# Routed experts as 48 pairs of 64-row half blocks on two column tiles of TensorE, in place of 63 blocks of 128 rows

## The chip, the cores and the metric

One core of one Trainium2 chip runs the kernel as one program. The metric is the device time of one execution in microseconds (us), as the median of several runs. In the profile the engines are PE (TensorE; PEld is its loading of stationary operands), DVE (VectorE), ACT (ScalarE), POOL (GpSimd) and SP (SyncE, which here issues DMAs).

## The reference

The model has two layers, each an attention part and a feed-forward part with layer norms around them, over 1024 tokens (2 x 512) of 256 features in fp32. The change touches only the last part, a mixture of experts:

```python
logits = x @ gate_w                              # 1024 x 32
topw, topi = jax.lax.top_k(softmax(logits), 4)   # 4 of 32 experts per token
topw = topw / topw.sum(-1, keepdims=True)
for each expert e:                               # wg, wu: 256 x 96; wd: 96 x 256
    h = silu(x @ wg[e]) * (x @ wu[e])
    out += combine[:, e:e+1] * (h @ wd[e])
out += sigmoid(x @ seg) * (silu(x @ sg) * (x @ su)) @ sd
```

So there are 1024 x 4 = 4096 pairs of a token and an expert, spread unevenly over 32 experts. How many fall to an expert is known only at run time.

## The kernel before, in words

The program is written engine by engine: each engine has its own list of instructions in program order, and semaphores tie the lists together (`wait_ge` before, `then_inc` after an instruction). `Chain.step` and `Chain.settle` (lines 57 to 80) make an engine wait for its own earlier results. Nothing is scheduled by a planner; the order in each list is the order of the source.

Up to about 488 us of the profile come the first layer, the second attention part, routing and the shared expert. Routing has these pieces. `route_top` takes the four best experts of each token. On TensorE `ranks` counts, for each token and expert, how many tokens come before it at that expert, and the totals. On VectorE `route_places` (L1224, once for each batch of 512 tokens) turns ranks and totals into a row number in the buffer `x_sorted` for each of the four copies of a token; `block_experts` (L1284) works out which expert each block of 128 rows belongs to, and this table goes through TensorE (`block_row`, L2051) into one row `etab` from which registers can be loaded. GpSimd scatters each token's row (256 features and 12 columns that say where the result is to go) four times into `x_sorted` (`scatter`, L779), after SP has filled that buffer with padding rows. Rows of one expert fill whole blocks of 128, so that 4096 / 128 + 31 = 63 blocks are enough for every distribution, and always 63 are run.

The stage of the blocks, in which the change lies, does this for each block i:

- SP (L605 to L610) loads 128 rows of 268 floats into `xblk`, four blocks ahead; it waits until the block four before is transposed and its ids are taken.
- TensorE `block_in` (L2057): two transposes of 128 x 128 into PSUM.
- VectorE `block_in` (L1354): copies the columns to `xcol` (L1359), and a small step (L1361) that finds which of the row's four copies this is; `block_ids` (L1365) reduces that to the row number `ids`.
- TensorE `block_up` (L2070): two matmuls (k = 0, 1), stationary `xcol` 128 x 128, moving the expert's 192 columns of `wgu`, at an address from a register. In fp32 each matmul is two instructions in the trace. The register is loaded by `value_load` (L2169), one block at a time.
- ScalarE `block_silu` (L1679) and VectorE `block_gate` (L1371) make the 128 x 96 hidden rows `hb`.
- TensorE `block_hidden` (L2084) transposes them, VectorE `block_hidden` (L1379) copies them to `hcol` (L1384).
- TensorE `block_down` (L2090): one matmul, stationary `hcol` 96 x 128, moving the expert's 256 columns of `wd`.
- ScalarE `block_out` (L1687) copies the result to `yblk`; GpSimd (L806 to L812) scatters its rows to `y_slots` by `ids`.

In one turn of its loop TensorE does `block_in(i)`, `block_up(i-1)`, `block_hidden(i-2)`, `block_down(i-3)`, and VectorE `block_in(i)`, `block_gate(i-1)`, `block_ids(i)`, `block_hidden(i-2)`. PSUM and SBUF tiles of a block are doubled (`i % 2`), and waits such as `pe.wait_ge(bt_copied, i - 1)` guard their reuse. After the last block the results are read back (`ycomb`), weighted and summed (`combine`, L1397).

The functions that the diff touches and what calls them:

## Time and profile before

| | us |
|---|---|
| median of 3 runs | 618.08 |
| runs | 617.88 to 623.02 |
| span of the profiled execution (first to last instruction) | 634.5 |
| of it, TensorE busy | 467.0 (74%) |
| of it, VectorE busy | 377.9 (60%) |
| of it, ScalarE busy | 263.8 (42%) |
| of it, GpSimd busy | 231.8 (37%) |

The profiled execution is another one than the timed runs; of it only the span is given. Busy times are sums over the span, and the kernel's stages have different limits, so a stage is read from its own window. Ends of matmuls are modelled in the trace, and a busy TensorE is not one at its peak. "<-" names what ended the idle time before an instruction; "issue" is time in which an engine waited for nothing that the profile shows.

### The profile page before, as it was taken

To read this page: it belongs to the slowest core of one execution; us is meant where nothing else is said; L and a number is where in the kernel's file an instruction comes from. 1 tells how busy PE (TensorE), PEld (TensorE's weight loads), DVE (VectorE), ACT (ScalarE), POOL (GpSimd) and SP (SyncE) were. 2 spreads that over 40 slices of the span, in tenths; PEclk is the share of its full clock that TensorE was granted. 3 is DMA by queue.
4 is the path that set the end of the run, shared out by engine and by line. 5 is a ranking of instruction groups with operands and counts; after the bars stand their busy time and mean duration, and the time that the engine had idled before them with its cause. 6 is when DMAs were issued, how large, how long until landed. Compare 5 with 4: busy or idle time off the path is not lost.

```text
span 634.5 us, 9931 instructions
## 1 busy us (share of the span) xinstructions
PE 467.0 (74%) x3183; PEld 342.9 (54%) x3183; DVE 377.9 (60%) x940; ACT 263.8 (42%) x507; POOL 231.8 (37%) x310
## 2 busy tenths in 40 slices
PE   2766888889886689798944445596785999999650
PEld 1544444444543377676734334484664878877440
DVE  6584577775671347655498839863712656665254
ACT  7317665664676342316711451423312434433202
POOL 5940323432548303203102211265170456565500
PEclk9957598996997769898987666997896999999776
DMA  6680521111410159300000006983022444543061
GB/s 191 156 164 22 84 44 40 39 31 30 143 38 3 67 161 337 110 1 1 1 1 25 25 25 141 256 251 113 18 104 61 125 133 126 150 137 98 11 265 66
DMA packets 56050, 60.16 MB, mean 95 GB/s; under 512 B 10420, under 2 KB 46909, under 8 KB 56000
## 3 DMA queue, kind: packets, MB, share of 16 engines
q1 hardware_dynamic: 50832, 50.79, 30.6%
q0 software_dynamic: 5168, 8.74, 4.1%
q8 instruction: 27, 0.44, 0.3%
q14 instruction: 23, 0.19, 0.1%
HBM read 37.67 MB, written 25.75 MB: 100 GB/s over the span
## 4 chain that ended last, share of the span: by engine, by line
PE 51%; DVE 21%; ACT 10%; issue 8%; DMA 4%; POOL 2%; another core or an unknown queue 2%; SPq 1%; POOLq 0%; DVEq 0%; ACTq 0%
PE ps L2076 8%; PE ps L1820 6%; PE ps L1799 5%; PE ps L2095 4%; PE ps L1870 4%; PE ps L1778 4%; ACT probs L1505 3%; PE ps L1858 3%; PE ps L1860 3%; PE ps L1859 3%; PE ps L2066 3%; DVE gain L1104 2%; DVE st L902 2%; PE ps L1832 2%; DVE h_lo L1061 2%
## 5 line engine op out<-in xcount | busy, mean ns | idle before, releaser
L1505 ACT ACTIVATE probs<-ps 128x512 f32<-128x512 f32 x160 | 86.9, 595 | 61.5 <-PE ps L1799 59.7
L809 POOL DMA_INDIRECT y_slots_scratch<-yblk,ids x63 | 62.0, 985 | 62.5 <-issue 28.8
L998 DVE TENSOR_REDUCE negm<-ps 128x2 f32<-128x1024 f32 (+1 forms) x64 | 67.1, 1080 | 26.3 <-PE ps L1788 26.1
L653 POOL TENSOR_TENSOR rstd<-ve,halfneg 128x4 f32<-128x4 f32 x16 | 16.6, 1036 | 132.0 <-DVE ve L933 79.6
L2076 PE MATMUL ps<-wgu,xcol 128*128 x252 | 58.5, 356 | 2.8 <-DVE xcol L1359 1.1
L1778 PE MATMUL ps<-k_all,q_ring 64*128 64x512 f32 (+3 forms) x256 | 52.9, 420 | 8.1 <-DVE negm L998 4.7
L1799 PE MATMUL ps<-q_ring,k_all 64*128 64x512 f32 (+3 forms) x256 | 44.2, 404 | 17.5 <-ACT probs L1505 17.5
L1820 PE MATMUL ps<-probs,v_all 128*32 128x128 f32 (+3 forms) x512 | 51.1, 499 | 5.2 <-POOL probs L698 2.8
L2076 PEld LDWEIGHTS ps<-wgu,xcol 128*128 128x128 f32 x252 | 40.3, 193 | 11.2 <-issue 8.4
L1545 ACT CAST h_hi<-hf 128x512 fp32r<-128x512 f32 x28 | 17.4, 620 | 66.7 <-DVE hf L1056 58.1
L1799 PEld LDWEIGHTS ps<-q_ring,k_all 64*128 64x128 f32 x256 | 23.3, 210 | 40.1 <-ACT probs L1505 30.2
L690 POOL TENSOR_TENSOR waited<-zero 128x1 f32<-128x1 f32 x48 | 9.3, 195 | 92.6 <-ACT probs L1505 92.6
L784 POOL DMA_INDIRECT x_sorted_scratch<-rows,dest x32 | 32.0, 1000 | 25.9 <-DVE dest L1282 16.7
L1778 PEld LDWEIGHTS ps<-k_all,q_ring 64*128 64x128 f32 x256 | 28.4, 218 | 23.7 <-issue 12.7
L1056 DVE TENSOR_TENSOR hf<-sg,ps 128x512 f32<-128x512 f32 x28 | 19.2, 684 | 36.5 <-PE ps L1860 13.2
L1001 DVE TENSOR_REDUCE negm<-ps 128x4 f32<-128x1024 f32 (+1 forms) x32 | 30.5, 959 | 16.0 <-PE ps L1788 15.9
L698 POOL TENSOR_SCALAR_AFFINE_SELECT probs<-probs 128x512 f32<-128x512 f32 x64 | 40.0, 637 | 0.0
L2095 PE MATMUL ps<-wd,hcol 96*128 x126 | 39.6, 398 | 0.4 <-DVE hcol L1384 0.3
L1376 DVE TENSOR_TENSOR hb<-gb,ps 128x96 f32<-128x96 f32 x63 | 16.0, 253 | 35.5 <-ACT gb L1684 23.6
L1684 ACT ACTIVATE gb<-ps 128x96 f32<-128x96 f32 x63 | 15.8, 251 | 45.0 <-PE ps L2076 37.1
L1359 DVE COPY xcol<-ps 128x256 f32<-128x256 f32 x63 | 26.6, 422 | 12.6 <-PE ps L2066 12.0
L1692 ACT COPY yblk<-ps 128x256 f32<-128x256 f32 x63 | 23.4, 372 | 23.9 <-PE ps L2095 19.6
(291 smaller groups left out, 1306.5 us busy)
## 6 DMA issues: line engine op xcount, KB each, us to landing
x_sorted_scratch<-pad SPq DMA_DIRECT2D x7, 1206.0 KB, 13.6
xblk<-x_sorted_scratch SPq DMA_DIRECT2D x63, 134.0 KB
wgu<-in_moe_w SPq DMA_DIRECT2D x4, 1536.0 KB
q_ring<-q_parts_scratch SPq DMA_DIRECT2D x64, 64.0 KB
ycomb<-y_slots_scratch SPq DMA_DIRECT2D x8, 512.0 KB, 7.0
wd<-in_moe_w SPq DMA_DIRECT2D x1, 3072.0 KB, 19.1
sraw<-in_moe_w SPq DMA_DIRECT2D x6, 384.0 KB, 3.5
q_parts_scratch<-qparts SPq DMA_DIRECT2D x4, 512.0 KB, 4.6
```

The lines of the kernel that those rows point to most:

```text
L698: pool.affine_select(out=tiles, in_=tiles, compare_op=ALU.is_ge, fill=0.0, base=0, pattern=[[0, GQ], [1, P]], channel_multiplier=-1).then_ ...
L784: pool.indirect_dma_start(out=x_sorted, out_offset=bass.IndirectOffsetOnAxis(ap=dest[:, u, j:j + 1], axis=0), in_=rows[:, u, :], in_offset ...
L809: pool.indirect_dma_start(out=y_slots, out_offset=bass.IndirectOffsetOnAxis(ap=ids[:, i:i + 1], axis=0), in_=yblk[:, i % YR, :], in_offset ...
L998: dve.tensor_reduce(negm[:, par, :, hp, qt], pair_of, AX.X, ALU.max, negate=True).then_inc(s1_read, 1)
L1001: dve.tensor_reduce(negm[:, par, :, :, qt], pair_of.rearrange("p a (h t) -> p a h t", h=nh), AX.X, ALU.max, negate=True).then_inc(s1_read, 1)
L1359: dve.tensor_copy(xcol[:, i % 2, :], ps[:, i % 2, 0:D]).then_inc(bt_copied, 1)
L1505: act.activation(probs[:, par, u, :], ps[:, col_unit(g, u), :], ACT.Exp)\
L1778: pe.matmul(ps[:, u % 2 * 2 + rg, end - w:end], q_ring[lane(rg, 64), g % QRING, h0 + h, qt * P:(qt + 1) * P], k_all[lane(rg, 64), g * T:g ...
L1799: mm = pe.matmul(ps[:, col_unit(g, 2 * p + rg), c:c + w], k_all[lane(rg, 64), g * T + kt * P:g * T + (kt + 1) * P], q_ring[lane(rg, 64), g ...
L1820: mm = pe.matmul(ps[32 * h:32 * h + 32, 7, kt * P:T], v_all[:, (g * TPB + kt) * 32:(g * TPB + kt + 1) * 32], probs[:, g % 2, un, c:c + T - ...
L2076: mm = pe.matmul(ps[:, 2 + i % 2, 0:2 * F].rearrange("p (w f) -> p w f", w=2), xcol[:, i % 2, k * P:(k + 1) * P], wgu[:, k, :, bass.ds(e * ...
L2095: pe.matmul(ps[:, 4 + i % 2, 0:D], hcol[0:F, i % 2, :], wd[0:F, bass.ds(e, 1), :].rearrange("p o d -> p (o d)"), start=True, stop=True).th ...
```

## The change

The unit of the buffer becomes a half block of 64 rows, and two half blocks make a pair that goes through the stage as a block did. Each of the 32 experts has one half block of its own, at a place known when the program is written; what an expert has beyond 64 rows goes to 64 free half blocks, whose experts are known at run time (`etab`). That is 96 half blocks, 48 pairs. Pair i has free half block i in rows 0 to 63. In rows 64 to 127 it has, for two pairs of three, the own half block of a fixed expert (`own_expert`), and for every third pair one of the last 16 free ones, whose weights ScalarE copies ahead to a fixed place (`copy_weights`).

- SP issues two loads of 64 rows for a pair (`first_rows`); padding takes 6 DMAs in place of 7.
- `block_up` and `block_down` on TensorE issue one matmul for each half: the stationary operand has 64 columns, the result goes to 64 partitions. The last pair has one expert and keeps the full width.
- Registers of four free half blocks are loaded at once, after `block_in` of every fourth pair. Waits that other waits imply are dropped.
- The order of a turn becomes, on TensorE, `block_in(i)`, (loads), `block_hidden(i-3)`, `block_up(i-1)`, `block_down(i-3)`, and on VectorE `block_in(i)`, `block_hidden(i-3)`, `block_gate(i-2)`, `block_ids(i)`; on ScalarE `block_silu(i-1)`, `block_out(i-3)`.
- `route_places` compares with 15 limits in place of 8 and has more steps (`to_own` among them).

The diff without its declarations, allocations and iotas, but for those of names that matter:

```diff
-BLOCKS = N * TOPK // P + E - 1
+HB = P // 2
+LIMITS = N // HB - 1
+FREE = N * TOPK // HB
+BLOCKS = (E + FREE) // 2
+TRIOS = BLOCKS // 3
...
+        def own_expert(i):
+            return None if i % 3 == 2 else i // 3 * 2 + i % 3
+        def first_rows(i):
+            own = own_expert(i)
+            return E * HB + i * HB, (E + BLOCKS + i // 3) * HB if own is None else own * HB
...
-                sp.dma_start(xblk[:, i % XR, :], x_sorted[i * P:(i + 1) * P, :])\
-                    .then_inc(xb_in[i % XR], 16)
+                for n, first in enumerate(first_rows(i)):
+                    sp.dma_start(xblk[half(n), i % XR, :], x_sorted[first:first + HB, :])\
+                        .then_inc(xb_in[i % XR], 16)
...
+            def to_own(rank):
+                chain.step(dve.scalar_tensor_tensor(
+                    pos[:, :, :], rank, float(HB),
+                    own[:, :].unsqueeze(1).to_broadcast((P, TPB, E)), ALU.is_lt, ALU.mult))
...
                 chain.step(dve.tensor_tensor(
-                    over[:, :, :], total.unsqueeze(2).to_broadcast((P, E, 8)),
-                    thr[:, :].unsqueeze(1).to_broadcast((P, E, 8)), ALU.is_gt))
+                    over[:, :, :], total.unsqueeze(2).to_broadcast((P, E, LIMITS)),
+                    thr[:, :].unsqueeze(1).to_broadcast((P, E, LIMITS)), ALU.is_gt))
                 if b == 1:
                     chain.step(dve.tensor_tensor(
                         late[:, :, :], rank, lim0[:, :].unsqueeze(1).to_broadcast(grid),
                         ALU.is_ge))
+                    to_own(rank)
                 chain.settle()
                 nb = (nb0, nb1)[b]
                 chain.step(dve.tensor_reduce(nb[:, :], over[:, :, :], AX.X, ALU.add))
...
                 if b == 0:
                     chain.step(dve.tensor_tensor_scan(in0[:, :], onesE[:, :], nb0[:, :], 0.0,
                                                       ALU.mult, ALU.add))
-                    chain.step(dve.tensor_scalar(lim0[:, :], nb0[:, :], float(P), None, ALU.mult))
-                    chain.settle()
-                    chain.step(dve.tensor_tensor(ex0[:, :], in0[:, :], nb0[:, :], ALU.subtract))
+                    chain.step(dve.tensor_scalar(lim0[:, :], nb0[:, :], float(HB), float(HB),
+                                                 ALU.mult, ALU.add))
                     chain.settle()
                     chain.step(dve.scalar_tensor_tensor(
-                        pos[:, :, :], ex0[:, :].unsqueeze(1).to_broadcast(grid), float(P), rank,
-                        ALU.mult, ALU.add))
+                        ex0[:, :], in0[:, :], float(E - 1), nb0[:, :], ALU.add, ALU.subtract))
+                    chain.settle()
+                    chain.step(dve.tensor_tensor(own[:, :], iota[:, :], ex0[:, :], ALU.subtract))
+                    chain.settle()
+                    to_own(rank)
+                    chain.settle()
+                    chain.step(dve.tensor_tensor(
+                        late[:, :, :], pos[:, :, :], ex0[:, :].unsqueeze(1).to_broadcast(grid),
+                        ALU.add))
                 else:
                     chain.step(dve.tensor_tensor(nb1[:, :], nb1[:, :], nb0[:, :], ALU.subtract))
                     chain.settle()
...
                         late[:, :, :], late[:, :, :],
                         ex0[:, :].unsqueeze(1).to_broadcast(grid), ALU.add))
                     chain.settle()
-                    chain.step(dve.scalar_tensor_tensor(
-                        pos[:, :, :], late[:, :, :], float(P), rank, ALU.mult, ALU.add))
+                    chain.step(dve.tensor_tensor(late[:, :, :], late[:, :, :], pos[:, :, :],
+                                                 ALU.add))
+                chain.settle()
+                chain.step(dve.scalar_tensor_tensor(
+                    pos[:, :, :], late[:, :, :], float(HB), rank, ALU.mult, ALU.add))
                 chain.settle()
                 shape = (P, TPB, TOPK, E)
...
-            for i in range(BLOCKS + 2):
+            for i in range(BLOCKS + 3):
                 if i < BLOCKS:
                     block_in(i)
-                if 0 <= i - 1 < BLOCKS:
-                    block_gate(i - 1)
+                if 0 <= i - 3 < BLOCKS:
+                    block_hidden(i - 3)
+                if 0 <= i - 2 < BLOCKS:
+                    block_gate(i - 2)
                 if i < BLOCKS:
                     block_ids(i)
-                if 0 <= i - 2 < BLOCKS:
-                    block_hidden(i - 2)
...
+            def copy_weights(c, e):
+                act.copy(wcopy[:, c % 2, :, :, :], wgu[:, :, :, bass.ds(e * F, F)])
+                act.copy(wdcopy[0:F, c % 2, :],
+                         wd[0:F, bass.ds(e, 1), :].rearrange("p o d -> p (o d)"))\
+                    .then_inc(w_copied, 1)
+            act.wait_ge(etab_ready, 1)
+            act.wait_ge(s_wd, 16)
+            act.wait_ge(s_wgu, 64)
+            for i in range(BLOCKS + 3):
+                if i % 8 == 1 and 8 <= i <= 33:
                     diagonal(*divmod(i // 8 - 1, 2))
-                if i < BLOCKS:
-                    block_silu(i)
-                if i >= 2:
-                    block_out(i - 2)
+                c = i // 3
+                if i % 3 == 0 and c < TRIOS - 1:
+                    copy_weights(c, act.value_load(etab[0:1, BLOCKS + c:BLOCKS + c + 1],
+                                                   min_val=0, max_val=E - 1))
+                if 0 <= i - 1 < BLOCKS:
+                    block_silu(i - 1)
+                if 0 <= i - 3 < BLOCKS:
+                    block_out(i - 3)
...
             def block_in(i):
-                pe.wait_ge(xb_in[i % XR], 16 * (i // XR + 1))
-                if i >= 2:
-                    pe.wait_ge(bt_copied, i - 1)
-                else:
+                pe.wait_ge(xb_in[i % XR], 32 * (i // XR + 1))
+                if i == 0:
                     pe.wait_ge(silu_done, B * (HC + SHARED))
                     pe.wait_ge(mul_done, B * (HC + SHARED))
                 for k in range(DC):
...
             def block_up(i, e):
+                own, c = own_expert(i), i // 3
                 pe.wait_ge(bt_copied, i + 1)
-                if i >= 2:
-                    pe.wait_ge(b_mul, i - 1)
+                if own is None and c < TRIOS - 1:
+                    pe.wait_ge(w_copied, c + 1)
                 for k in range(DC):
-                    mm = pe.matmul(
-                        ps[:, 2 + i % 2, 0:2 * F].rearrange("p (w f) -> p w f", w=2),
-                        xcol[:, i % 2, k * P:(k + 1) * P], wgu[:, k, :, bass.ds(e * F, F)],
-                        start=k == 0, stop=k == DC - 1)
+                    cols = xcol[:, i % 2, k * P:(k + 1) * P]
+                    up = ps[:, 2 + i % 2, 0:2 * F].rearrange("p (w f) -> p w f", w=2)
+                    free = wgu[:, k, :, bass.ds(e * F, F)]
+                    if i == BLOCKS - 1:
+                        mm = pe.matmul(up, cols, free, start=k == 0, stop=k == DC - 1)
+                    else:
+                        second = (wcopy[:, c % 2, k, :, :] if own is None
+                                  else wgu[:, k, :, own * F:(own + 1) * F])
+                        pe.matmul(up[half(0)], cols[:, half(0)], free, start=k == 0,
+                                  stop=k == DC - 1)
+                        mm = pe.matmul(up[half(1)], cols[:, half(1)], second, start=k == 0,
+                                       stop=k == DC - 1)
                 mm.then_inc(bu_done, 1)
             def block_hidden(i):
                 pe.wait_ge(b_mul, i + 1)
-                if i >= 2:
-                    pe.wait_ge(bh_copied, i - 1)
                 pe.transpose(ps[0:F, 6 + i % 2, 0:P], hb[:, i % 2, :], ident[:, :])\
                     .then_inc(bh_done, 1)
             def block_down(i, e):
+                own, c = own_expert(i), i // 3
                 pe.wait_ge(bh_copied, i + 1)
                 if i >= 2:
                     pe.wait_ge(by_ready, i - 1)
-                pe.matmul(ps[:, 4 + i % 2, 0:D], hcol[0:F, i % 2, :],
-                          wd[0:F, bass.ds(e, 1), :].rearrange("p o d -> p (o d)"),
-                          start=True, stop=True).then_inc(bd_done, 1)
+                free = wd[0:F, bass.ds(e, 1), :].rearrange("p o d -> p (o d)")
+                if i == BLOCKS - 1:
+                    mm = pe.matmul(ps[:, 4 + i % 2, 0:D], hcol[0:F, i % 2, :], free,
+                                   start=True, stop=True)
+                else:
+                    pe.matmul(ps[half(0), 4 + i % 2, 0:D], hcol[0:F, i % 2, half(0)], free,
+                              start=True, stop=True)
+                    mm = pe.matmul(ps[half(1), 4 + i % 2, 0:D], hcol[0:F, i % 2, half(1)],
+                                   wdcopy[0:F, c % 2, :] if own is None else wd[0:F, own, :],
+                                   start=True, stop=True)
+                mm.then_inc(bd_done, 1)
...
             for i in range(BLOCKS + 3):
                 if i < BLOCKS:
                     block_in(i)
+                    if i % 4 == 0:
+                        _, loaded = nc.values_load_multi_w_load_instructions(
+                            etab[0:1, i:i + 4], engines=[mybir.EngineType.PE], min_val=0,
+                            max_val=E - 1)
+                        experts.update(enumerate(loaded, i))
+                if 0 <= i - 3 < BLOCKS:
+                    block_hidden(i - 3)
                 if 0 <= i - 1 < BLOCKS:
-                    experts[i - 1] = pe.value_load(etab[0:1, i - 1:i], min_val=0, max_val=E - 1)
                     block_up(i - 1, experts[i - 1])
-                if 0 <= i - 2 < BLOCKS:
-                    block_hidden(i - 2)
                 if 0 <= i - 3 < BLOCKS:
                     block_down(i - 3, experts.pop(i - 3))
...
```

## Rows read from the trace of the kernel before

**Rows 1.** Page, first line and busy times in 40 slices of the span.
```profile
span 634.5 us, 9931 instructions
...
PE   2766888889886689798944445596785999999650
...
PEclk9957598996997769898987666997896999999776
```
**Rows 2.** Chain that ended last, 480 to 600 us: start us, us, what.
```profile
488.25 0.42 PE ps L2066 x2
488.70 0.43 DVE xcol L1359
...
489.35 1.64 PE ps L2076 x4
...
577.14 1.56 PE ps L2066 x2
...
583.34 1.54 PE ps L2087
...
594.42 0.97 PE ps L2076 x4
...
598.41 0.38 ACT yblk L1692
```
**Rows 3.** Timeline of one block: start us, us, engine, line, operation, count.
```profile
540.58 0.38 PE L2066 MATMUL ps<-ident,xblk 128*128 128x128 f32 x2
...
540.92 0.91 PE L2076 MATMUL ps<-wgu,xcol 128*128 x4
...
541.00 0.42 DVE L1359 COPY xcol<-ps 128x256 f32<-128x256 f32 x1
541.34 0.21 DVE L1361 SCALAR_TENSOR_TENSOR xblk<-xblk,placf 128x4 f32<-128x4 f32 x1
...
541.67 0.27 PE L2087 MATMUL ps<-ident,hb 128*96 128x128 f32 x1
...
541.78 0.60 PE L2095 MATMUL ps<-wd,hcol 96*128 x2
...
542.21 0.38 PE L2066 MATMUL ps<-ident,xblk 128*128 128x128 f32 x2
```
**Rows 4.** Busy time in a window: PE, PEld, DVE, ACT, POOL, clock, DMA, GB/s.
```profile
520.00:560.00 40.00, 39.42 (x224) 32.45 (x224) 25.40 (x123) 17.33 (x58) 24.20 (x26) 1.00 0.52 140
```
**Rows 5.** Attention: timeline of TensorE, then L1820 and L1778 there, ns min/median/max.
```profile
102.04 0.86 PE L1820 MATMUL ps<-probs,v_all 128*32 128x256 f32 x16
102.83 0.50 PE L1778 MATMUL ps<-k_all,q_ring 64*128 64x512 f32 x2
...
L1820 PE MATMUL ps<-probs,v_all x16: 272/326/403, 102.0 to 102.6; 128*32 128x256 f32 x8, 128*32 128x128 f32 x8
...
L1778 PE MATMUL ps<-k_all,q_ring x4: 386/445/497, 102.8 to 103.6; 64*128 64x512 f32 x4
```
**Rows 6.** Timeline, a down product that waited, and VectorE's steps one behind another.
```profile
584.75 0.31 PE L2087 MATMUL ps<-ident,hb 128*96 128x128 f32 x1
...
584.90 0.29 DVE L1384 COPY hcol<-ps 96x128 f32<-96x128 f32 x1
...
585.33 0.69 PE L2095 MATMUL ps<-wd,hcol 96*128 x2 [0.27 <-DVE hcol L1384]
...
585.67 0.42 DVE L1359 COPY xcol<-ps 128x256 f32<-128x256 f32 x1 [0.48 <-remote]
...
586.01 0.21 DVE L1361 SCALAR_TENSOR_TENSOR xblk<-xblk,placf 128x4 f32<-128x4 f32 x1
...
586.18 0.25 DVE L1376 TENSOR_TENSOR hb<-gb,ps 128x96 f32<-128x96 f32 x1
```
**Rows 7.** Line L2169 on TensorE's sequencer: ns min/median/max, first and last start.
```profile
L2169 PEldq TENSOR_LOAD <-etab x63: 296/303/522, 488.4 to 593.6; - x63
...
L2169 PEldq SEQ_ASSERT  x63: 18/18/28, 489.2 to 594.1; - x63
```
**Rows 8.** Chain that ended last: the first step of each route_places.
```profile
390.99 0.43 DVE over L1231
...
450.83 0.33 DVE over L1231
```
**Rows 9.** Groups by form on VectorE, 450 to 457 us: busy us, mean ns.
```profile
L1275 DVE TENSOR_TENSOR eq<-eq,pos 128x512 f32<-128x512 f32 x1 | 0.7, 691 | 0.0
...
L1231 DVE TENSOR_TENSOR over<-ps,thr 128x256 f32<-128x256 f32 x1 | 0.4, 416 | 0.0
```
**Rows 10.** Single lines: ns min/median/max; and one group of the page (mean ns).
```profile
L1692 ACT COPY yblk<-ps x63: 360/372/378, 494.4 to 598.4; 128x256 f32<-128x256 f32 x63
...
L609 SPq DMA_DIRECT2D xblk<-x_sorted_scratch x63: 319/319/433, 478.2 to 586.6; - x63
...
L1505 ACT ACTIVATE probs<-ps 128x512 f32<-128x512 f32 x160 | 86.9, 595 | 61.5 <-PE ps L1799 59.7
```

More of the change, by code:

```diff
@@ L228, in sandwich_kernel @@
         wgu_at = mhi_at - 2 * E * F * 4
+        (wcopy, wdcopy), end = place(
+            region, ("wcopy", [P, 2, DC, 2, F], F32), ("wdcopy", [P, 2, D], F32))
+        assert end <= half_q
         (wgu,), _ = place(wgu_at, ("wgu", [P, DC, 2, E * F], F32))
@@ L798, in _ @@
                 chunk_low(c)
[L799 removed]
+            pool.wait_ge(s_sorted, 6 * 16)
             scatter(0)
@@ L1210, in block_constants @@
             def block_constants():
-                dve.wait_ge(s_const2, 6)
+                dve.wait_ge(s_const2, 7)
                 chain.step(dve.memset(rows[:, :, D + TOPK:XW], 0.0))
-                chain.step(dve.tensor_copy(placf[:, :], placi[:, :]))
+                chain.step(dve.tensor_scalar(placf[half(0), :], placi[half(0), 0:BLOCKS],
+                                             float(E * HB), None, ALU.add))
+                second = placf[half(1), :].rearrange("p (g m) -> p g m", m=3)
+                chain.step(dve.tensor_scalar(
+                    second[:, :, 0:2],
+                    placi[half(1), BLOCKS:].rearrange("p (g m) -> p g m", m=3)[:, :, 0:2],
+                    float(-HB), None, ALU.add))
+                chain.step(dve.tensor_scalar(second[:, :, 2], placi[half(1), 0:TRIOS],
+                                             float((E + BLOCKS - 1) * HB), None, ALU.add))
                 chain.settle()
```

43 lines of the change are left out of this document (24 added, 19 removed).

## The prediction

> **What bounds the kernel now.** I read the chain of waits first, then the timeline of one block, then the windows by stage. The chain passes through the routed experts from 488.25 us (first transposes of block 0) to 598.41 us (last copy of an output block): 110 of 634.5 us, and in it nearly every step is TensorE's [rows 1, 2]. From the first block's up product (489.35) to the last one's (594.42) lie 62 blocks in 105.1 us, 1.69 us each. One block undisturbed is 540.92 to 542.48, 1.56 us: up product 0.75 to the next instruction, the transpose of the hidden rows 0.11, the down product 0.43, the two transposes of the next block 0.27 [rows 3]. So 62 x 1.56 = 96.7 us are the pace of TensorE and 8.4 us are not: they sit in the cold first blocks and in some ten places where a step of the chain takes 1 to 1.5 us instead of 0.3 (577.14 and 583.34 are two) [rows 2]. In 520 to 560 TensorE is busy 39.42 of 40 us at clock 1.00, VectorE 25.40, ScalarE 17.33, GpSimd 24.20 [rows 4]. TensorE is what a block costs; the others have room.
>
> **The change, step 1: fewer passes.** 48 pairs replace 63 blocks. At 1.56 us each that would take away 15 x 1.56 = 23.4 us. This is the most that the change can give, and it holds only if a pair costs what a block costs.
>
> **Step 2: do two halves of 64 columns run side by side?** A pair issues twice the matmuls for the up and the down product. The trace has fp32 column tiles already: in attention (L1820) 16 instructions of four 32-column tiles, 8 of width 256 and 8 of width 128, begin at 102.04, and the next work begins at 102.83 [rows 5]. A 256-wide instruction streams in 0.215 (two downs take 0.43 [rows 3]), so one after another they would need 8 x 0.215 + 8 x 0.107 = 2.6 us; they took 0.7 to 0.8. Four ran at once. I take two halves as side by side: up 4 x 0.162 = 0.65, down 2 x 0.215 = 0.43, as now. Not side by side they would add 0.65 + 0.43 = 1.08 us a pair.
>
> **Step 3: what a pair adds on TensorE.** Column tiles alternate with full-width transposes, twice a pair. In the same place the work after the column tiles begins 0.07 us before the modelled end (102.04 + 0.86) of the last of them; that one is 128 wide, lasts 0.27 as recorded, streams 0.107, so 0.10 us pass with nothing streaming. Then its weights have to be loaded in the open: L1778 lasts 497 ns there against 386 in the middle of its run, 0.11 us for 128 columns [rows 5]; for 64 columns I estimate half, 0.055, and for a transpose 0.05 (the hidden transpose that waited lasts 0.31 against 0.27 [rows 3, 6]). TensorE alone: three transposes 0.05 + 0.33, gap 0.10, up 0.055 + 0.65, down 0.43, gap 0.10: 1.72 us.
>
> **Step 4: the wait that takes over.** The new order is transposes(i), hidden(i-3), up(i-1), down(i-3) on TensorE, and on VectorE columns(i), ids step, hidden copy(i-3), gate(i-2), ids(i). The down product now waits for a hidden copy made in the same turn, and VectorE makes that copy only behind the column copy, which waits for the turn's transposes. Before, hidden copy and down product were one turn apart. The loop, from the turn's start: second transpose begins at 0.16, its recorded end is 0.27 later (0.43); the column copy begins 0.04 after that (540.96 to 541.00), 0.47; the next VectorE step 0.34 later, 0.81; the one behind it 0.17 later, which is the hidden copy, 0.98 [rows 3, 6]; from the start of a hidden copy to the down product that waited for it are 0.43 (584.90 to 585.33) [rows 6], 1.41; weights 0.055, first of the two rounds 0.215, so the last begins at 1.68; the next turn's transposes begin 0.07 before its recorded end of 0.38, at 1.99. So a pair costs 1.99 us and not 1.72: TensorE is ready for the down product at 1.19 and waits 0.22. Behind the waiting product stand the next transposes, and VectorE waits for those: that is why the wait is paid in full.
>
> **Step 5: register loads.** Now every block reads its expert's number (L2169): a load of 0.30 us, an operation of 0.15 and a check, 0.5 us from the load's start to the check in the last block, 0.8 in the first [rows 7]; it passes while TensorE works off what is queued. The change loads four at a time, after the transposes of every fourth pair and ahead of the hidden transpose. The queue behind it is free when the down product of the turn before has been let go, at about 1.41, and the hidden transpose may come as late as 0.62 into the next turn without delaying the hidden copy (0.98 less 0.04, 0.27 and 0.05), so 1.99 + 0.62 - 1.41 = 1.20 us are free. What four cost the trace doesn't show: at least one (0.5), at most four in a row (4 x 0.8 = 3.2). I take one load and four times the rest of it at an estimated 0.27: 1.4 us, 0.2 over, 12 times: 2.4 us. At the low end 0, at the high end 12 x 2.0 = 24 us.
> The Trainium skill (Runtime: NRT & Kernel Launch, Instruction fetch mechanics) gives about 200 ns for each register loaded, in bulk too. By it the four would need 0.8 us of loading instead of 0.30, and the sum would be 12 x 0.5 = 6 us higher. No run here shows more than one register in a load; the one that the rows show took 0.30.
>
> **Step 6: ahead of the stage.** Both calls of route_places lie on the chain (from 390.99 and 450.83) [rows 8]. Limits go from 8 to 15: the comparison and its sum go from 256 to 480 elements; 0.42 us at 256 and 0.69 at 512 [rows 9] make 0.24 more each, 0.475 per call. The first call gets three more dependent steps (one of 32 elements, 0.2; two of 128, 0.3 each, with the settle between them 0.86); the second one step beside another (0.2) and one dependent (0.32). Together 1.33 + 1.0 = 2.3 us, all on the path: the table of experts and the destinations wait for it.
>
> **Step 7: what I cost at nothing.** ScalarE copies weights for every third pair: 384 elements, between 0.37 (256) and 0.60 (512) [rows 10], 0.37 more, and a register load; some 1.5 us on every third turn beside 0.25 + 0.37 each turn, against 1.99, and the gate has a turn's slack more than before. Without that cover it would cost 15 x 0.2 = 3 us. VectorE's five steps last 1.32 us of 1.99. GpSimd's scatter (0.98) comes 48 times in place of 63. SP issues 96 loads of 64 rows at 0.32 each [rows 10], 0.64 a turn, four turns ahead. The removed waits on TensorE free its queue, which the wait of step 4 makes worth nothing.
>
> **The sum.** 47 turns x 1.99 = 93.5, and 2.4 for register loads: 95.9 against 96.7. I leave the 8.4 us of irregular time and the stage's ends as they are: 104.3 against 105.1, -0.8. With +2.3 ahead of it: +1.5 us. The profiled execution, whose span is 634.5, would come to 636.0; only its span is given, and it is 16.4 us above the median of the runs (618.08), so some of its stalls may be the profiler's. On the median: 619.6.
>
> **The rivals.**
> A, faster: the hidden copy is not waited for, and TensorE's own 1.72 us sets the pace. For it: VectorE has 0.67 us free in a turn, and some turns may find columns copied early. Against it: the order on VectorE is fixed. 47 x 1.72 = 80.8; the register loads then find less cover (0.93 free, 12 x 0.47 = 5.6): 86.4 + 8.4 + 2.3 against 105.1 is -8.0: 610.
> B, faster: the irregular 8.4 us shrink with 15 fewer scatters and shorter loads. All of it gone: 611.
> C, slower: four loads cost four times one. At 0.65 each, 2.6 us: 1.4 over, 12 times 16.8 in place of 2.4: 634. It decides from about 1.8 us per group of four, where the total is +1%.
> D, slower: the halves run side by side only in part (the two instructions of one half hold up the next half): up 0.82 and down 0.64, some 0.2 us more a turn: 629. If not at all, 47 x 0.8 more: 657, against rows 5.
> E, slower: each late step now meets a loop without slack and costs twice: +8: 628.
>
> **How the numbers follow.** Within 1% (a measurement of this kernel can tell about 1%, 6 us, from no change): my forecast, 0.50. A 0.13 and B 0.07: faster 0.20. C 0.15, D 0.08, E 0.07: slower 0.30. The forecast's own range, from a turn of 1.93 to 2.08 and 0 to 6 us of register loads, is 615 to 627. The range given takes in A and B and reaches up to C: 608 to 634; outside are a full A with less irregular time, D without any overlap, and the high end of step 5.
>
> **What would show it.** Right: in the stage the turn is 1.9 to 2.1 us; TensorE's idle time before the first instruction of the down product is put down to the hidden copy, in nearly every turn; up instructions start in twos some ns apart; the full clock holds. Step 5: every fourth turn longer by some tenths. Step 6: the stage begins 2 to 3 us later if nothing else moves. Wrong: a turn of 1.75 (A) or over 2.3 (C, D), up products of 0.8 us and more, a clock below 1.00 within the stage, ScalarE's copies ahead of the gate as what VectorE waits for.

## The result

Over 20 runs each, the changed kernel takes 622.02 us against 619.60 us for the kernel before on the same chip; the ratio is 1.0045, with a 95% interval of 1.0023 to 1.0067. The forecast was 619.6 us and "within 1%". Medians here and below are of all runs, ratios leave the slow ones out (here two of the changed kernel, at 628 and 629 us). The profiled execution of the kernel before, on which the prediction rests, has a span of 634.5 us [rows 1]; another execution of the same kernel (first experiment below) has 618.2. The profiled execution of the changed kernel takes 620.25 us and has a span of 618.5.

The page of the changed kernel, first line and slices, answers to [rows 1]; its window answers to [rows 4], with the same columns:

```profile
span 618.5 us, 9821 instructions
...
PE   2766888898886779798965244777777899999650
...
PEclk9957599999898769898996576898789899999866
```
```profile
520.00:560.00 40.00, 36.71 (x289) 19.27 (x285) 19.19 (x97) 18.32 (x58) 18.68 (x19) 1.00 0.39 107
```

In the same window TensorE is busy 36.71 us in place of 39.42, VectorE 19.19 in place of 25.40, GpSimd 18.68 in place of 24.20. These three have more room than before, ScalarE (18.32 in place of 17.33) is still idle more than half the time, the granted clock is 1.00, and yet the stage takes no less time: something that is no engine's load sets the pace. One turn, in the timeline of the changed kernel (start us, us, engine, line, operation), answers to [rows 3]:

```profile
506.75 0.44 PE L2132 MATMUL ps<-ident,xblk 128*128 128x128 f32 x2
...
507.02 0.27 PE L2160 MATMUL ps<-ident,hb 128*96 128x128 f32 x1
...
507.22 0.42 DVE L1412 COPY xcol<-ps 128x256 f32<-128x256 f32 x1 [1.09 <-PE ps L2132]
507.23 0.38 PE L2151 MATMUL ps<-wgu,xcol 128*64 x1
...
507.23 0.38 PE L2153 MATMUL ps<-wgu,xcol 128*64 128x192 f32 x1
...
507.56 0.21 DVE L1414 SCALAR_TENSOR_TENSOR xblk<-xblk,placf 128x4 f32<-128x4 f32 x1
...
507.70 0.28 DVE L1437 COPY hcol<-ps 96x128 f32<-96x128 f32 x1
...
507.76 0.33 PE L2151 MATMUL ps<-wgu,xcol 128*64 x1
...
508.11 0.13 PEld L2174 LDWEIGHTS ps<-wd,hcol 96*64 96x64 f32 x1 [0.36 <-issue]
508.12 0.42 PE L2174 MATMUL ps<-wd,hcol 96*64 x1
...
508.70 0.33 PE L2132 MATMUL ps<-ident,xblk 128*128 128x128 f32 x1
```

A turn is 506.75 to 508.70, 1.95 us. The reader is to follow the loop: transposes, column copy at 507.22, the small step at 507.56, the hidden copy at 507.70, and only then, at 508.12, the down product (L2174), though the last up instruction (L2151) began at 507.76 and the rounds of an up product follow one another in 0.16. The view puts the idle time of the weight load down to "issue" and not to the hidden copy; the order of the starts points to the wait, and an experiment below (hidden copy first) shows it.

Every fourth turn is longer. These rows are the turn with the register load, then the load's line on TensorE's sequencer (ns min/median/max), which answers to [rows 7]:

```profile
512.60 0.44 PE L2132 MATMUL ps<-ident,xblk 128*128 128x128 f32 x2
...
513.58 0.31 PE L2160 MATMUL ps<-ident,hb 128*96 128x128 f32 x1 [0.54 <-issue]
...
514.52 0.38 PE L2174 MATMUL ps<-wd,hcol 96*64 x1
...
515.05 0.44 PE L2132 MATMUL ps<-ident,xblk 128*128 128x128 f32 x2
```
```profile
L2251 PEldq FUSED_REGOPS  x48: 146/148/165, 480.1 to 571.8; - x48
...
L2251 PEldq TENSOR_LOAD <-etab x12: 328/332/533, 479.5 to 570.6; - x12
```

The hidden transpose comes 0.98 after the transposes in place of 0.27, and the turn lasts 2.45. Eleven turns are of this kind, 2.43 to 2.62, 2.52 in the mean; the others are 1.95 from the fourth on. The 47 intervals make 98.0 us.

### The profile page after: what moved, and what is told of

The parts are those of the page before. It is cut to its first block, busy times and chain, and to the rows that moved or that the text cites. A ratio compares the mean times of both kernels' runs of the same rounds, so it can differ in the third digit from the quotient of the medians.

```text
span 618.5 us, 9821 instructions
## 1 busy us (share of the span) xinstructions
PE 450.1 (73%) x3330; PEld 305.7 (49%) x3330; DVE 364.1 (59%) x872; ACT 266.8 (43%) x507; POOL 217.9 (35%) x296
## 4 chain that ended last, share of the span: by engine, by line
PE 47%; DVE 21%; issue 11%; ACT 10%; POOL 7%; DMA 3%; SPq 1%; POOLq 0%; DVEq 0%; ACTq 0%
PE ps L2151 6%; PE ps L1888 6%; PE ps L1867 5%; PE ps L2174 4%; PE ps L1846 4%; POOL x_sorted_scratch L812 4%; ACT probs L1558 3%; PE ps L2132 3%; PE ps L1938 3%; PE ps L1926 2%; DVE st L930 2%; PE ps L1927 2%; PE ps L1928 2%; PE ps L1900 2%; DVE gain L1132 2%
## 5 line engine op out<-in xcount | busy, mean ns | idle before, releaser
L837 POOL DMA_INDIRECT y_slots_scratch<-yblk,ids x48 | 47.2, 984 | 64.0 <-ACT yblk L1745 56.9
L1888 PE MATMUL ps<-probs,v_all 128*32 128x128 f32 (+3 forms) x512 | 48.4, 476 | 5.7 <-DVE att L1054 2.9
L1412 DVE COPY xcol<-ps 128x256 f32<-128x256 f32 x48 | 20.4, 424 | 53.7 <-PE ps L2132 53.7
L2151 PE MATMUL ps<-wgu,xcol 128*64 x188 | 41.9, 347 | 0.0
L1089 DVE TENSOR_TENSOR h_lo<-hf,h_hi 128x512 fp32r<-128x512 f32 x28 | 20.9, 745 | 19.2 <-ACT h_hi L1598 16.5
L1852 PE MATMUL ps<-hide_swap,swapped 64*128 64x128 bf16 x128 | 31.7, 247 | 0.0
L1852 PE MATMUL ps<-hide_cols,identb 64*128 64x128 bf16 x128 | 31.7, 247 | 0.0
L2174 PE MATMUL ps<-wd,hcol 96*64 x94 | 29.6, 397 | 1.2 <-DVE hcol L1437 0.5
L1737 ACT ACTIVATE gb<-ps 128x96 f32<-128x96 f32 x48 | 11.9, 247 | 41.9 <-PE ps L2153 26.8
```

Source lines behind the costliest of these rows:

```text
L837: pool.indirect_dma_start(out=y_slots, out_offset=bass.IndirectOffsetOnAxis(ap=ids[:, i:i + 1], axis=0), in_=yblk[:, i % YR, :], in_offset ...
L1852: pe.matmul(ps[:, u % 2 * 2 + rg, end - P:end], own[lane(rg, 64), :], masks[lane(rg, 64), :], start=False, stop=False)
L1888: mm = pe.matmul(ps[32 * h:32 * h + 32, 7, kt * P:T], v_all[:, (g * TPB + kt) * 32:(g * TPB + kt + 1) * 32], probs[:, g % 2, un, c:c + T - ...
L2151: pe.matmul(up[half(0)], cols[:, half(0)], free, start=k == 0, stop=k == DC - 1)
L2174: pe.matmul(ps[half(0), 4 + i % 2, 0:D], hcol[0:F, i % 2, half(0)], free, start=True, stop=True)
```

## The experiments

All times are medians, ratios are against the kernel before on the same chip. "Stage" is the time from the first transpose of the stage to the end of the last copy of an output block; a turn or interval is the time from one block's transposes to the next one's.

| run | us | ratio [95%] | stage us | turn us |
|---|---|---|---|---|
| before, again (first) | 619.97 (one run) | | 103.0 | 1.54 median, 1.58 mean |
| changed kernel | 622.02 | 1.0045 [1.0023, 1.0067] | 104.7 | 1.95, with load 2.52 |
| hidden copy first | 614.54 | 0.9934 [0.9911, 0.9958] | 96.5 | 1.71, with load 2.3 to 2.8 |
| single loads | 615.93 | 0.9932 [0.9897, 0.9966] | 98.3 | 1.95 |
| both | 610.62 | 0.9853 [0.9784, 0.9922] | 92.9 | 1.83 mean |
| whole blocks | 615.94 | 0.9922 [0.9878, 0.9967] | 99.3 | 1.84, with load 2.3 to 2.7 |
| before, fewer waits | 611.86 | 0.9862 [0.9782, 0.9942] | 94.9 | 1.42 median, 1.45 mean |
| load ahead | 605.84 | 0.9746 [0.9679, 0.9813] | 88.8 | 1.71, 1.75 mean |
| half after half | 622.27 (one run) | | 105.1 | 1.95 |
| whole, load ahead | 596.53 | 0.9659 [0.9602, 0.9716] | 79.4 | 1.49 median, 1.55 mean |
| two per switch | 632.01 | 1.0143 [1.0074, 1.0212] | 112.1 | 3.1 to 7.5 for two |
| two per switch, deep | 602.43 | 0.9709 [0.9683, 0.9735] | 82.5 | 3.12 for two |

**The kernel before once more**, unchanged.

> The kernel before, unchanged, for a second profile. My theory: its late steps (8.4 us in the stage) and the 10.6 us stall ahead of the stage belong to that one profiled execution; then the span is about 616 to 618, the stage of the blocks begins at about 480 (set by the scatter of rows, not by the shared expert) and lasts about 102 us at 1.56 to 1.60 us a block. Rival: they belong to the kernel; then the span is again over 630 and the 62 intervals take 105 us.

Stage 478.77 to 581.77, 103.0 us, against 110.5 in the profile on record (488.25 to 598.79 [rows 2]). The 62 intervals take 98.0 us, not 105.1. The irregular 8.4 us of the prediction belonged mostly to that one execution: 98.0 against 96.7 leaves 1.3 us of it. And 62 intervals of before now cost exactly what 47 turns of after cost, 98.0 us.

**Is it the hidden copy that the down product waits for?** The hidden copy is put ahead of the column copy on VectorE, nothing else:

```diff
             for i in range(BLOCKS + 3):
-                if i < BLOCKS:
-                    block_in(i)
                 if 0 <= i - 3 < BLOCKS:
                     block_hidden(i - 3)
+                if i < BLOCKS:
+                    block_in(i)
```

> The changed kernel with one move on VectorE: the hidden copy of pair i-3 stands ahead of the column copy of pair i in a turn. My theory (step 4: the down product waits for a hidden copy that stands behind the column copy): the hidden copy begins at 0.58 in the turn and not at 0.98, the down product is ready at 1.01, TensorE is not before 1.19, so three turns of four go from 1.955 to about 1.72. The turn with the four register loads keeps less cover and is longer by some 0.8 and not 0.55: a group of four takes 7.7 us and not 8.37, 8 us in all: about 614. Rival: the pace is set elsewhere (drains between tile modes, ScalarE's copies): the group stays at 8.4 and the time at 622.

The timeline of one turn of it:

```profile
508.18 0.44 PE L2132 MATMUL ps<-ident,xblk 128*128 128x128 f32 x2
...
508.76 0.29 DVE L1437 COPY hcol<-ps 96x128 f32<-96x128 f32 x1 [0.73 <-PE ps L2160]
...
508.97 0.41 DVE L1412 COPY xcol<-ps 128x256 f32<-128x256 f32 x1
...
509.36 0.38 PE L2174 MATMUL ps<-wd,hcol 96*64 x1
...
509.89 0.44 PE L2132 MATMUL ps<-ident,xblk 128*128 128x128 f32 x2
```

The hidden copy now starts 0.58 after the transposes in place of 0.95, the down product 1.18 in place of 1.37, and the turn is 1.71 to the hundredth. Two exchanged steps on an engine that is half idle give 8.2 us of stage. The load turns now stand out more, since the flat turn covers less.

**What do four registers at once cost?** The load of one number at a time, ahead of its up product, as in the kernel before:

```diff
-                    if i % 4 == 0:
-                        _, loaded = nc.values_load_multi_w_load_instructions(
-                            etab[0:1, i:i + 4], engines=[mybir.EngineType.PE], ...)
-                        experts.update(enumerate(loaded, i))
                 if 0 <= i - 1 < BLOCKS:
+                    experts[i - 1] = pe.value_load(etab[0:1, i - 1:i], min_val=0, max_val=E - 1)
                     block_up(i - 1, experts[i - 1])
```

> The changed kernel with its registers loaded one at a time, directly ahead of the up product, as before the change. My theory (step 5): one load with its check takes 0.72 us on TensorE's queue and has 0.9 to 1.0 us of cover there (from the release of the down product at 1.41 to the up product at 2.4), so every turn is 1.955 and the 0.55 us in every fourth turn are gone: 12 x 0.55 = 6.6 us, about 615.5. Rival: loads cost by their number wherever they stand, 48 x 0.3 us or more are added: over 630.

Every turn is 1.95 from the fourth on and none longer: 48 single loads cost nothing that shows, 12 fourfold ones the 6.3 us by which the stage is now shorter. The sequencer's records in the changed kernel show why (start us, ns, what, without the checks of 18 ns; line L2174 is the down product before, L2151 the up product behind):

```
511.918  46 FUSED_REGOPS L2174
512.058 330 TENSOR_LOAD  L2251
512.446 151 FUSED_REGOPS L2251
512.732 151 FUSED_REGOPS L2251
...
513.298 146 FUSED_REGOPS L2251
513.599  51 FUSED_REGOPS L2151
```

The load begins when the down product is let go, 1.41 after the turn's start (510.65). The load itself takes 0.33 us for four numbers, against 0.30 for one [rows 7]; each number then costs 0.28 more on the sequencer. In all it is 1.51 us until the hidden transpose's weights at 513.57.

**Both edits together.**

> Both moves together. My theory: every turn at TensorE's own 1.72 us, flat: 47 x 1.72 = 81 us in place of 98, about 604 to 605, below the kernel before. Rival: one of the two covers is used up by the other (the load of 0.72 ends at 1.74, the up product is wanted at 2.1), or another engine sets the pace at 1.9: 611 or more.

It missed: 610.62 and a mean turn of 1.83. The two gains use one cover. With a turn of 1.71 a load between the hidden transpose and the up product starts only when the gate is through, and the up product begins 0.20 to 0.48 us after the hidden transpose in place of 0.20 to 0.24.

**The load ahead of the hidden transpose**, still one number a turn (the edit is against the version with both edits):

```diff
+                if 0 <= i - 1 < BLOCKS:
+                    experts[i - 1] = pe.value_load(etab[0:1, i - 1:i], min_val=0, max_val=E - 1)
                 if 0 <= i - 3 < BLOCKS:
                     block_hidden(i - 3)
                 if 0 <= i - 1 < BLOCKS:
-                    experts[i - 1] = pe.value_load(etab[0:1, i - 1:i], min_val=0, max_val=E - 1)
                     block_up(i - 1, experts[i - 1])
```

> The changed kernel with the hidden copy ahead of the column copy on VectorE, and with one register loaded in each turn, ahead of the hidden transpose and not behind it. Theory: in the run with both edits the load stood behind the wait of the hidden transpose (released at about 1.49 of a turn of 1.71), so 0.72 us of loading ended after the up product could have started. Ahead of the hidden transpose it begins when the down product is let go, at 0.87, and ends at 1.6, before the hidden transpose is due at 1.98: every turn 1.71 to 1.75, stage 87 to 89 us, 604 to 606 us. Rival (the sequencer has too much to issue in 1.71 us wherever the load stands): turns of 1.80 and more, 609 to 611 us, as with the load behind.

605.84 us, stage 88.8, nearly every turn 1.71: against the version with both edits only the place of the load differs, so the place decided there. Against "hidden copy first" only the grouping differs, one number a turn in place of four every fourth turn at the same place, and the stage is 88.8 in place of 96.5 us: the grouping costs by itself. This version does all the work of the changed kernel and beats both: 0.9746 of before.

**Do the halves run side by side because they alternate?** The up product's instructions are ordered first half k = 0, 1, then second half k = 0, 1 in place of by turns.

> The changed kernel, with the up product's instructions in the order first half k = 0, first half k = 1, second half k = 0, second half k = 1, in place of alternating halves. Result and work are the same. It asks how the halves come to run side by side. Theory 1 (each tile is fed on its own, so the second half's stream starts without waiting for the first half's): nothing changes, turn 1.95, 622 us. Theory 2 (instructions start in order, so the second half begins only when the first half's last one streams): the up product takes seven rounds of 0.162 in place of four, 1.13 us, and ends 0.27 us behind the time at which the down product could start: turn about 2.2, some 13 us more: 635 us.

```profile
509.10 0.38 PE L2149 MATMUL ps<-wgu,xcol 128*64 x1
509.12 0.38 PE L2155 MATMUL ps<-wgu,xcol 128*64 128x192 f32 x1
509.31 0.33 PE L2149 MATMUL ps<-wgu,xcol 128*64 x1
509.33 0.33 PE L2155 MATMUL ps<-wgu,xcol 128*64 128x192 f32 x1
```

L2149 is the first half, L2155 the second, in this run's timeline: though all of L2149 stands ahead of L2155 in the list, they start 0.02 us apart and pass each other. Nothing changed in the time.

**What do the two tiles cost?** Each pair as one whole block, so the second half's own expert is left out:

```diff
-                    if i == BLOCKS - 1:
+                    if True:
                         mm = pe.matmul(up, cols, free, start=k == 0, stop=k == DC - 1)
...
-                if i == BLOCKS - 1:
+                if True:
                     mm = pe.matmul(ps[:, 4 + i % 2, 0:D], hcol[0:F, i % 2, :], free, ...)
```

> The changed kernel, but each of the 48 pairs is multiplied as one whole block of 128 rows: one instruction of 128 columns in place of two halves of 64, in the up and in the down product. The second half's own expert is left out (its rows go through the first half's expert). Waits, register loads, copies and transfers stay. It prices the two column tiles. Theory (the loop of step 4 sets the turn; the tiles cost it only what stands behind the down product): the down product still starts at about 1.37 to 1.40 us of the turn, lasts 0.43, and no 0.10 us of drain follows it: turn 1.82 in place of 1.95, every fourth again 0.55 longer, stage some 6 us shorter: about 616 us. Rival 1 (the tiles cost nothing): turn 1.95, 622. Rival 2 (the tiles are what makes a pair slower than a block): turn 1.56, about 603.

The turn fell to 1.84 and the time to 615.94, as the theory had it:

```profile
531.25 0.38 PE L2132 MATMUL ps<-ident,xblk 128*128 128x128 f32 x2
...
532.14 0.28 DVE L1437 COPY hcol<-ps 96x128 f32<-96x128 f32 x1
...
532.56 0.69 PE L2171 MATMUL ps<-wd,hcol 96*128 x2 [0.17 <-DVE hcol L1437]
...
533.09 0.38 PE L2132 MATMUL ps<-ident,xblk 128*128 128x128 f32 x2
```

Whole blocks still wait for the hidden copy, and here the view names it. So of the 0.4 us by which a pair's turn is longer than a block's the halves make 0.11; the most of it is the loop through VectorE.

The same edit in the version with the load ahead, where TensorE itself sets the turn:

> The version with the hidden copy first and one register load a turn ahead of the hidden transpose, but with each pair multiplied as one whole block of 128 rows (the second half's own expert is left out). It prices the two column tiles where TensorE itself sets the turn. Theory: the halves cost 1.71 less 1.42, the interval that 63 whole blocks reached without the spare waits: some 0.29 us a pair for draining twice and loading the first weights in the open. Turn 1.42 to 1.45, stage about 76 us, 592 us. Rival (with 1.42 us VectorE or the sequencer is the bound at once, so the tiles cost less than 0.29 in truth): turn 1.55 to 1.65, 597 to 602 us.

596.53 us, median turn 1.49, between the two: the tiles cost at least 0.22 us a pair there. It need not be all, since a part of the 1.49 is TensorE's list and not its array: every third turn takes 1.55, and these are the turns in whose list stands the wait for ScalarE's copied weights (L2141), which takes 0.05 us and 0.106 until the next step. At a turn of 1.71 or 1.95 the same wait doesn't show. Against 63 blocks at 1.42 (the next experiment) the price would be 0.29.

**What were the removed waits worth by themselves?** In the kernel before, with its 63 blocks, the three waits that the change also takes out:

```diff
-                if i >= 2:
-                    pe.wait_ge(bt_copied, i - 1)
-                else:
+                if i < 2:
...
-                if i >= 2:
-                    pe.wait_ge(b_mul, i - 1)
...
-                if i >= 2:
-                    pe.wait_ge(bh_copied, i - 1)
```

> The kernel before, with 63 blocks, without the three waits on TensorE that the change takes out as well (columns copied in block_in, gate multiplied in block_up, hidden copied in block_hidden, each from i = 2). It tells what that part of the change is worth by itself. Theory: before, TensorE's sequencer is short of time: a register load every block and seven waits; the streamed work of a block is about 1.45 us and the interval 1.54 to 1.58. Without the three waits the interval falls to 1.45 to 1.50: 62 times 0.1, some 6 us: 613 us. Rival (waits already passed cost nothing, as step 7 of the prediction has it): the interval stays 1.54 to 1.58, 619 us.

611.86 us, 0.9862 of before, and most intervals are 1.42. The timeline of one block of it, against 540.58 to 542.21 in [rows 3]:

```profile
540.36 0.38 PE L2064 MATMUL ps<-ident,xblk 128*128 128x128 f32 x2
540.58 0.81 PE L2072 MATMUL ps<-wgu,xcol 128*128 x4
541.23 0.27 PE L2081 MATMUL ps<-ident,hb 128*96 128x128 f32 x1
541.34 0.60 PE L2089 MATMUL ps<-wd,hcol 96*128 x2
541.77 0.38 PE L2064 MATMUL ps<-ident,xblk 128*128 128x128 f32 x2
```

The up product now takes 0.65 to the next instruction, not 0.75. In the unchanged kernel these waits stand on the sequencer as follows (one of the three, ns min/median/max):

```profile
L2074 PEldq EVENT_SEMAPHORE  x61: 51/51/51, 483.4 to 578.1; - x61
```

Each is implied by an earlier wait in the same list and so can't hold anything up, but each takes 0.05 us and some 0.11 to 0.125 until the next step of the list. Some 0.12 of the 1.54 us of a block were thus the list and not the array. This part of the change, alone and with 63 blocks, is faster than the whole change (0.9862 of before against 1.0045).

**Half as many changes of tiling.** The version with the load ahead, with two pairs in a turn and one load of two numbers: four transposes and two hidden transposes on the whole array, then two up and two down products in halves; VectorE and ScalarE go in twos, and `xcol` has four buffers.

```diff
-            for i in range(BLOCKS + 3):
+            for g in range(0, BLOCKS + 4, 2):
...
+                    block_in(g)
+                    block_in(g + 1)
...
+                    block_hidden(g - 4)
+                    block_hidden(g - 3)
...
+                    block_up(g - 2, experts[g - 2])
+                    block_up(g - 1, experts[g - 1])
...
+                    block_down(g - 4, experts.pop(g - 4))
+                    block_down(g - 3, experts.pop(g - 3))
```

> The same version, with two pairs in each turn: four transposes and two hidden transposes on the whole array, then two up and two down products in halves, so that TensorE changes between whole array and column tiles half as often; VectorE and ScalarE take their steps in twos, the columns have four buffers in place of two, and one load brings two registers. Theory: each change of tiling costs about 0.14 us (drain and open weight load), so a pair costs 0.14 less: double turn of 3.13 us, 24 of them, stage some 7 us shorter: 598 to 600 us. Rival 1 (the 0.29 us are paid by each half product, not by the change): double turn 3.42, 606 us. Rival 2 (the longer chain through VectorE and ScalarE, or the two-register load, takes the place): double turn over 3.5, 608 us and more.

None of the three: 632.01, slower than before. The transposes' line names a cause (us of idle time, times, weight loads and matmuls counted apart):

```profile
  DMA xblk<-x_sorted_scratch: 22.8, 27
```

The matmuls alone are 13 of the 27, with 11.3 us, 3.8 of it ahead of the stage; in the chain that ended last, transfers of rows and their issue on SP make 34% of 480 to 593 us. A turn takes two blocks of rows at once, the buffers hold four, and a new load starts only when the ids of a block four back are taken. Besides, behind a late transpose the load of two numbers holds up the hidden transposes (idle before them, "issue", 11.2 us in 16 times). Seven buffers, ids ahead of the gates, and two single register loads (one ahead of the down products) mend it together; what each of the three does alone was not run:

> The version with two pairs a turn once more, with what held it up taken away: seven input buffers in place of four (TensorE waited for input rows at 27 transposes), the token numbers worked out ahead of the gates on VectorE, and two single register loads a turn, one ahead of the down products, one behind the transposes, in place of one load of two. Theory (each change of tiling costs some 0.14 us, and the last run was slow for its transfers alone; its undisturbed double turns were 3.12): double turn 3.12 to 3.2, stage some 83 us, 599 to 601 us. Rival (the chain through VectorE and ScalarE or the register loads still set the turn): double turn 3.4 to 3.6, 606 to 612 us.

```profile
530.75 0.66 PE L2130 MATMUL ps<-ident,xblk 128*128 128x128 f32 x4
531.55 0.48 DVE L1436 COPY hcol<-ps 96x128 f32<-96x128 f32 x2 [1.01 <-PE ps L2158]
...
532.90 0.38 PE L2172 MATMUL ps<-wd,hcol 96*64 x1
...
533.87 0.66 PE L2130 MATMUL ps<-ident,xblk 128*128 128x128 f32 x4
```

The double turn is 3.12 from one end of the stage nearly to the other, 1.56 a pair in place of 1.71. If the saved changes of tiling were all that the grouping saves, two changes would cost 0.30 us, near the 0.29 above and over the 0.22; buffers and loads differ too, so 0.22 to 0.30 is what the runs show. The time, 602.43, is 1.4 us above the upper end expected, though the stage of 82.5 us is as expected. It is the fastest version here with the whole computation.

## Why the prediction was right, point by point

**What bounds the kernel** was half right. TensorE set the pace of a block, but in part by its list of instructions and not by its array: without three waits that were already passed a block takes 1.42, not 1.54. So the pairs were set against a block that could itself be 0.12 faster, and a pair of 1.56 or 1.71 is never as cheap as such a block, though 47 turns of 1.56 still take less than 62 intervals of 1.42 (73 against 88 us).

**Steps 1 and 2** hold. 15 passes fewer came, and the halves run side by side: starts 0.01 apart, and the rounds of an up product follow one another in 0.16 as before.

**Step 3** holds: TensorE alone was put at 1.72 and is 1.71 where nothing waits (hidden copy first). Its part for the tiles, two gaps of 0.10 and weights in the open, is 0.22 to 0.30 by the runs with whole blocks and with two pairs in a turn. The Trainium skill (TensorEngine Tiling (Array Packing), Tiling Modes) has it that a change of tiling mode drains the array, without a price; the price of a change that the runs show here fits it.

**Step 4** carried the forecast and holds: turn 1.95 for 1.99, down product at 1.37 for 1.41, put down to the order on VectorE, which the exchange of two steps showed. The sign named for it failed in part: the views of the changed kernel call most of this idle time "issue".

**Step 5 is the term that was mis-sized**: "1.4 us, 0.2 over, 12 times: 2.4 us". The load begins at 1.41 as told and lasts 1.51, near 1.4. The cover was wrong: "the hidden transpose may come as late as 0.62 into the next turn" looks at VectorE alone. Behind the hidden transpose stands the up product, and TensorE had only the 0.22 us of step 4 to spare, so the transpose may come 0.27 + 0.22 = 0.49 into the turn. The cover is then 1.95 + 0.49 - 1.41 = 1.03 in place of 1.20, and 1.51 is 0.48 over; the eleven turns are 0.57 longer in the mean, 6.2 us, where 2.4 was told for twelve (the first load falls into the uneven opening of the stage).
The Trainium skill's price (Runtime: NRT & Kernel Launch, Instruction fetch mechanics), 200 ns for each register also in bulk, isn't seen here: four took 0.33 us to load, one 0.30 (the page speaks of loads from HBM, and `etab` lies in SBUF). What each number costs is 0.28 of register operations behind the load.

**Step 6** holds in its sizes and not in its path: on VectorE route_places grew by 1.35 and 0.98 us, told as 1.33 and 1.0. First step of the first call, a wait between the calls, first and last step of the second call, before again and then changed:

```profile
388.52 0.42 DVE L1231 TENSOR_TENSOR over<-ps,thr 128x256 f32<-128x256 f32 x1
...
414.47 1.29 DVE L917 TENSOR_TENSOR rows<-ps,bo_sb 128x512 f32<-128x512 f32 x2 [2.18 <-PE ps L1982]
...
448.27 0.42 DVE L1231 TENSOR_TENSOR over<-ps,thr 128x256 f32<-128x256 f32 x1
...
452.88 0.17 DVE L1282 CAST dest<-destf 128x16 uint32<-128x16 f32 x1
```
```profile
387.25 0.66 DVE L1274 TENSOR_TENSOR over<-ps,thr 128x480 f32<-128x480 f32 x1
...
413.08 1.29 DVE L945 TENSOR_TENSOR rows<-ps,bo_sb 128x512 f32<-128x512 f32 x2 [0.69 <-PE ps L2050]
...
447.03 0.65 DVE L1274 TENSOR_TENSOR over<-ps,thr 128x480 f32<-128x480 f32 x1
...
452.62 0.17 DVE L1335 CAST dest<-destf 128x16 uint32<-128x16 f32 x1
```

The prediction had both "all on the path". From call to call pass 59.75 and 59.78 us: what the first call grew by was taken up where VectorE waits for TensorE, 0.69 in place of 2.18 us. From the second call's first step to the stage are 30.50 and 32.49 us: 0.98 more by the call, 0.16 by the scatter behind it, 0.85 by the loads of step 7. So 2.0 us reach the stage, near the 2.3 told, but by half through a term that was put at nothing. The other nine versions with pairs have 31.7 to 32.4 us in the same stretch, before with fewer waits 30.6. The stage begins only 0.75 later (478.77, 479.52), because the first call began 1.27 earlier in the changed kernel's execution.

**Step 7** holds at a turn of 1.95 but for the loads of rows. The copies of weights had ScalarE's room, and behind the second pair (1.11 us) no transposes waited for rows. But a load of 64 rows keeps SP busy for 0.60 us in the median, not 0.32:

```profile
L633 SPq DMA_DIRECT2D xblk<-x_sorted_scratch x96: 444/596/1192, 476.3 to 571.2; - x96
```

A pair needs two, and so the first transposes begin 3.24 us after the first load of rows (476.28 to 479.52) in place of 2.39 (476.38 to 478.77).

**The sum.** Told were 95.9 us for the changed kernel's intervals against 96.7, 8.4 us of irregular time on both sides and 2.3 ahead. Measured are 98.0 against 98.0: the turns 47 x 0.04 = 1.9 below, the register loads and the opening turns 3.9 above (98.0 less 47 x 1.95 is 6.3), the irregular time absent on the one side and 1.3 us on the other. Errors of 2 to 8 us, of both signs or alike on both sides, left the difference at 622.02 - 619.60 = 2.4 us where 1.5 was told: that VectorE's order holds the turn near 1.95 was understood, that the sum came so close is partly luck. It can't be checked closer either: the two profiled executions differ by 0.3 us in span, with 1.7 more in the stage, a start 0.75 later, and 2.1 less from the last output copy to the end (36.4 and 34.3; 33.9 to 36.7 over all profiles).

**The rivals.** A: 1.72 was TensorE's own pace, but the order on VectorE kept it away; the exchange of two steps brought it. B and E: the irregular time was not there to shrink or to double. C: four numbers cost 1.51, not 2.6. D: the halves overlap in full.

## What to carry to other kernels

When a change makes one engine's work shorter, draw the new loop through the other engines first: here TensorE and VectorE had more room than before and the pace was set by a chain of four steps, which two exchanged lines shortened by 0.24 us a turn. Count the instruction list of an engine as a resource of its own: waits that are already passed and register operations take 0.1 to 0.3 us of it each, which costs time where the list runs just ahead of the array, and a cover for them is the shortest slack of all that is queued behind, not that of one engine. Group the work by tiling mode, with input buffers deep enough for the larger group.

## What was not expected

Three waits a block that were already passed cost 62 x 0.13 us, 1.4% of the time. A load of 64 rows keeps SP busy for longer (0.60 us) than one of 128 rows did (0.32). One load brings four registers in 0.33 us, one in 0.30, but each costs 0.28 more behind it, so fewer and larger register loads were the worse choice. And the second tile's instructions overtook those of the first that stood ahead of them, by 0.5 us of streaming, with nothing lost.
